# Graph layer with two branches: the first loads of x2 and adj cut finer, the warm-up shortened, and the opening lists of ScalarE and VectorE reordered

## What is computed

```python
def conv(x, a, eps, W, b):            # three layers
    ax = a @ x
    h = ax + (1.0 + eps[0]) * ax
    for i in range(3):
        h = relu(h @ W[i].T + b[i])
    return h
h = maximum(layernorm(x), 0.0)
out1 = conv(h,  adj, eps1, W1, b1)    # branch 0
out2 = conv(x2, adj, eps2, W2, b2)    # branch 1
return x + concatenate((out1, out2), axis=1) @ Wm.T + bm
```

## Time and profile before

| | |
|---|---|
| three runs | 405.01, 405.08, 406.11 us; median 405.08 |
| the profiled execution | 404.87 us, of which the traced span is 403.3 us |
| TensorE matmul | 399.4 us busy, 99% of the span, 1757 instructions |
| TensorE weight load | 327.0 us, 81% |
| VectorE, ScalarE | 219.6 us (54%), 220.4 us (55%) |
| DMA | 76.22 MB, mean 189 GB/s; above 400 GB/s in the first slices of the span |

### The profile page before, as it was taken

How to read it: one execution, slowest core, us unless ns; L and a number is a source line. 1 busy time by engine, 2 the same in 40 slices (tenths; PEclk the granted TensorE clock), 3 DMA queues, 4 the chain that set the end, 5 groups by cost and what they waited for, 6 DMA issues and landing times.

```text
span 403.3 us, 4833 instructions
## 1 busy us (share of the span) xinstructions
PE 399.4 (99%) x1757; PEld 327.0 (81%) x1757; DVE 219.6 (54%) x267; ACT 220.4 (55%) x258; POOL 8.4 (2%) x19
## 2 busy tenths in 40 slices
PE   8999999999999999999999999999999999999997
PEld 3788888888888888888888888888888888888886
DVE  5898878656464434551645517345373444755223
ACT  6876868557574533555433556334564335766034
POOL 0000000000000000000100001000000000000100
PEclk9999999999999999999999999999999999999999
DMA  8998883744645165334574336653175551740100
GB/s 301 420 403 338 310 327 142 297 154 152 236 154 198 53 244 203 108 119 197 172 296 160 119 137 228 240 207 132 76 260 208 208 193 42 264 179 2 52 0 28
DMA packets 14030, 76.22 MB, mean 189 GB/s; under 512 B 1920, under 2 KB 2176, under 8 KB 6080
## 3 DMA queue, kind: packets, MB, share of 16 engines
q1 hardware_dynamic: 12240, 71.18, 46.9%
q0 software_dynamic: 1200, 3.93, 2.9%
q10 hardware_dynamic: 576, 0.92, 0.7%
HBM read 73.93 MB, written 2.10 MB: 189 GB/s over the span
## 4 chain that ended last, share of the span: by engine, by line
PE 99%; DVE 0%; issue 0%; DVEq 0%
PE acc L590 24%; PE acc L586 24%; PE acc L587 24%; PE second_acc L587 3%; PE second_acc L586 3%; PE second_acc L590 3%; PE hidden L590 3%; PE hidden L586 3%; PE hidden L587 3%; PE second_acc L604 2%; PE acc L604 2%; PE merged L756 1%; PE acc L618 1%; PE merged L590 1%; PE merged L586 1%; PE merged L587 1%
## 5 line engine op out<-in xcount | busy, mean ns | idle before, releaser
L586 PE MATMUL acc<-adj_hi,feat_lo 128*128 128x512 f32 x432 | 168.0, 389 | 0.0
L587 PE MATMUL acc<-adj_hi,feat_hi 128*128 128x512 f32 x432 | 168.0, 389 | 0.0
L590 PE MATMUL acc<-adj_lo,feat_hi 128*128 128x512 f32 x432 | 168.0, 389 | 0.0
L423 DVE TENSOR_TENSOR adj_lo<-adj_raw,adj_hi 128x2048 fp32r<-128x2048 f32 x48 | 108.4, 2289 | 37.5 <-ACT adj_hi L264 36.6
L264 ACT ACTIVATE adj_hi<-adj_raw 128x2048 fp32r<-128x2048 f32 x48 | 90.3, 1924 | 17.3 <-PE acc L590 15.4
L429 DVE TENSOR_TENSOR act_lo<-act_f,act_hi 128x512 fp32r<-128x512 f32 x60 | 41.1, 691 | 104.4 <-ACT act_f L284 104.3
L587 PEld LDWEIGHTS acc<-adj_hi,feat_hi 128*128 128x128 f32 x432 | 81.1, 188 | 16.9
L590 PEld LDWEIGHTS acc<-adj_lo,feat_hi 128*128 128x128 f32 x432 | 81.1, 188 | 16.9
L586 PEld LDWEIGHTS acc<-adj_hi,feat_lo 128*128 128x128 f32 x432 | 81.1, 188 | 16.7
L283 ACT ACTIVATE act_hi<-hidden,bias 128x512 fp32r<-128x512 f32 x45 | 30.9, 688 | 95.5 <-PE hidden L590 95.5
L483 DVE TENSOR_TENSOR adj_lo<-adj_raw,adj_hi 128x2048 fp32r<-128x2048 f32 x14 | 31.7, 2290 | 5.4 <-ACT adj_hi L302 5.4
(11 more groups left out here) (82 smaller groups left out, 224.1 us busy)
## 6 DMA issues: line engine op xcount, KB each, us to landing
adj_raw<-adj_tiles SPq DMA_DIRECT2D x62, 1024.0 KB, 5.3
x_rows<-x_tiles SPq DMA_DIRECT2D x16, 256.0 KB, 7.3
x_res<-x_t POOLq DMA_DIRECT2D x8, 256.0 KB, 6.1
out_t<-y_sb POOLq DMA_DIRECT2D x7, 256.0 KB, 2.3
adj_raw<-adj_second SPq DMA_DIRECT2D x2, 512.0 KB, 6.5
adj_raw<-adj_first ACTq DMA_DIRECT2D x3, 256.0 KB, 4.4
w_raw<-w_t SPq DMA_DIRECT2D x1, 512.0 KB, 5.6
adj_raw<-adj_first SPq DMA_DIRECT2D x1, 256.0 KB, 5.0
```

Source lines behind the costliest of these rows:

```text
L423: nc.vector.tensor_tensor(adj_lo[:, u % RING, :], adj_raw[:, u % RING, :], f32(adj_hi[:, u % RING, :]), ALU.subtract).then_inc(lo_made, 1)
L586: nc.tensor.matmul(out, lhs_lo, rhs_hi, start=start, stop=False)
L587: nc.tensor.matmul(out, lhs_hi, rhs_hi, start=False, stop=False)
L590: return nc.tensor.matmul(out, lhs_hi, rhs_lo, start=False, stop=stop)
```

## The change

It cuts two of the first loads. Of x2's unit 0 the first block (128x128, 64 KB) gets a DMA and a semaphore of its own (`first_x2_loaded`), the other three blocks (192 KB) another. The first piece of adj is loaded in two halves by partitions, partitions 64 to 127 on SP's queue (`upper_loaded`), 0 to 63 on ScalarE's (`fine_loaded0`). x comes behind x2 on SP's queue, and the third piece of adj's first unit goes to ScalarE's queue, the fourth to SP's. Five of the twelve warm-up matmuls go. The lists of ScalarE and VectorE are reordered in the opening; the matmuls of TensorE keep their order, and the second of the raw ones now waits for the rest of x2.

```diff
--- before.py
+++ after.py
@@ -35,7 +35,7 @@
 
     PIECES = ((1, 1, 1, 1), (2, 2))
     X_SLOTS = 4
-    WARM_UP = 12
+    WARM_UP = 7
     HALF = JB // 2
 
 
@@ -131,6 +131,8 @@
         raw_loaded = [sem(f"raw_loaded{s}") for s in range(RING)]
         fine_loaded = [sem(f"fine_loaded{i}") for i in range(sum(len(p) - 1 for p in PIECES))]
         x_loaded = [sem(f"x_loaded{s}") for s in range(X_SLOTS)]
+        first_x2_loaded = sem("first_x2_loaded")
+        upper_loaded = sem("upper_loaded")
         x2_loaded = [sem(f"x2_loaded{s}") for s in range(X_SLOTS)]
         w_loaded = sem("w_loaded")
         bias_loaded = sem("bias_loaded")
@@ -214,9 +216,12 @@
                 sp.dma_start(x2_rows[:, u % X_SLOTS], x2_tiles[u]).then_inc(x2_loaded[u % X_SLOTS], 16)
 
 
+
+            sp.dma_start(x2_rows[:, 0, 0], x2_tiles[0, :, 0]).then_inc(first_x2_loaded, 16)
+            sp.dma_start(adj_raw[P // 2:P, 0, 0:CW], adj_first[0, P // 2:P]).then_inc(upper_loaded, 16)
+            sp.dma_start(x2_rows[:, 0, 1:JB], x2_tiles[0, :, 1:JB]).then_inc(x2_loaded[0], 16)
             load_x(0)
-            load_x2(0)
-            for s, i in ((0, 2), (1, 0), (1, 1)):
+            for s, i in ((0, 3), (1, 0), (1, 1)):
                 to, piece_of, done = piece_load(s, i)
                 sp.dma_start(to, piece_of).then_inc(done, 16)
             for s, (u, c) in enumerate(OPENING):
@@ -302,6 +307,8 @@
                 nc.scalar.activation(adj_hi[:, s % RING, :], adj_raw[:, s % RING, :], ACT.Copy).then_inc(hi_made, 1)
 
             def high_of_x2(u):
+                if u == 0:
+                    act.wait_ge(first_x2_loaded, 16)
                 act.wait_ge(x2_loaded[u % X_SLOTS], 16 * (u // X_SLOTS + 1))
                 nc.scalar.activation(feat_hi[:, 1, u * JB:(u + 1) * JB, :], x2_rows[:, u % X_SLOTS],
                                      ACT.Copy).then_inc(feat2_hi_made, 1)
@@ -332,26 +339,28 @@
                                      ACT.Copy).then_inc(feat1_hi_made, 1)
 
 
-            for i in (0, 1, 3):
+            act.dma_start(adj_raw[0:P // 2, 0, 0:CW], adj_first[0, 0:P // 2]).then_inc(fine_loaded[0], 16)
+            for i in (1, 2):
                 to, piece_of, done = piece_load(0, i)
                 act.dma_start(to, piece_of).then_inc(done, 16)
             act.wait_ge(constants_made, 2)
             nc.scalar.activation(root_of_zero[:, :], zero[:, :], ACT.Sqrt)
 
+            act.wait_ge(upper_loaded, 16)
             piece_high(0, 0)
-            std_of_x(0)
             piece_high(0, 1)
             high_of_x2(0)
+            std_of_x(0)
+            piece_high(0, 2)
+            piece_high(0, 3)
             act.wait_ge(rstd_made, 1)
             rectify_half(0, half_relu_made, half_feat1_made)
-            piece_high(0, 2)
-            piece_high(0, 3)
             rectify_half(1, relu_made, feat1_hi_made)
             piece_high(1, 0)
             piece_high(1, 1)
             high_of_x2(1)
+            high_of_opening(2)
             std_of_x(1)
-            high_of_opening(2)
             high_of_opening(3)
             rectify(1)
             for u in range(2, U - 2):
@@ -485,6 +494,8 @@
 
             def low_of_x2(u):
                 rows = slice(u * JB, (u + 1) * JB)
+                if u == 0:
+                    dve.wait_ge(first_x2_loaded, 16)
                 dve.wait_ge(x2_loaded[u % X_SLOTS], 16 * (u // X_SLOTS + 1))
                 dve.wait_ge(feat2_hi_made, u + 1)
                 nc.vector.tensor_tensor(feat_lo[:, 1, rows, :], x2_rows[:, u % X_SLOTS], f32(feat_hi[:, 1, rows, :]),
@@ -500,20 +511,21 @@
             nc.vector.memset(zero[:, :], 0.0).then_inc(constants_made, 1)
             nc.vector.memset(ln_eps[:, :], LN_EPS).then_inc(constants_made, 1)
 
+            dve.wait_ge(upper_loaded, 16)
+            piece_low(0, 0)
             variances(0)
+            piece_low(0, 1)
             scale_and_shift(0)
-            piece_low(0, 0)
-            piece_low(0, 1)
-            low_of_x2(0)
             piece_low(0, 2)
             piece_low(0, 3)
-            variances(1)
+            low_of_x2(0)
             low_of_x(0)
             piece_low(1, 0)
+            variances(1)
             piece_low(1, 1)
             low_of_x2(1)
+            low_of_opening(2)
             scale_and_shift(1)
-            low_of_opening(2)
             low_of_opening(3)
             low_of_x(1)
             for u in range(2, U - 2):
@@ -609,10 +621,14 @@
 
                 u, c = OPENING[s]
                 out = opening_bank(c, first)
-                pe.wait_ge(x2_loaded[u], 16)
+                if s == 0:
+                    pe.wait_ge(first_x2_loaded, 16)
+                    pe.wait_ge(upper_loaded, 16)
                 for i in pieces:
                     js, n = piece(s, i)
                     pe.wait_ge(raw_loaded[s] if n is None else fine_loaded[n], 16)
+                    if (s, i) == (0, 1):
+                        pe.wait_ge(x2_loaded[u], 16)
                     for j in js:
                         slot, cols = columns(s, j)
                         last = nc.tensor.matmul(out[:, :], x2_rows[:, u, j, :], adj_raw[:, slot, cols],
```

## The result

| | before | changed |
|---|---|---|
| median of 14 runs, us | 404.98 | 406.09 |
| lowest to highest | 404.67 to 406.11 | 405.55 to 406.35 |
| profiled execution, us | 404.87 | 406.17 |
| its span | 403.3 | 404.6 |
| TensorE matmul busy | 399.4 | 400.0 |

The ratio is 1.0022, 95% interval 1.0015 to 1.0029: 0.6 to 1.2 us slower, 0.9 in the middle (the medians stand 1.1 apart). That is less than the 0.3% I had set for a change, and more than the 0.1 us of the forecast.

The account below looks back on a forecast made before the run. TensorE bounds the kernel, 99% of the span. A 2.2 us earlier start leaves 1.1, spent waiting on x's late chain: 16.41 - 16.30 = +0.1 on 404.87 gives 405.0, plus 0.2 for the median, 405.2; range 404.0 to 406.2.

Parts of the forecast that it names:

- one named wait: TensorE's last two matmuls on chunk 1 wait for VectorE's second low: start at 16.41 instead of 16.30, +0.1 us.
- the working of 10.06 us: VectorE's chain from the start of x's statistics at 6.35 to TensorE's load behind the second low at 16.41.
- later lows: VectorE's lows after chunk 1: ready at 19.4 and 22.7, wanted at 20.3 and 23.0, so costed at nothing.
- the ring of adj: Slots for adj's loads, asked for at most 1 us later by SP, behind queued transfers: costed at nothing.
- The statistics start at 6.35.: VectorE's statistics of x, 4.29 before, wait for x behind 384 KB on SP's queue; bounds 6.1 and 7.3.
- The rival of the small transfers: Two additional issues hold x back 0.46 us each: statistics at 7.3, low at 17.35, time 406.1; chance 18%.
- I let the clock rise at the same instant: TensorE's clock goes from 1.2 to 2.4 GHz at about 6.65 as before, so the first split product could start at 10.55.
- the 1.1 us that the start was to leave: TensorE's raw matmuls start 2.2 us earlier; 1.1 is left at the first split product, the rest spent at the lower clock.
- Their data come in time.: adj's pieces for the raw matmuls: fourth in at 7.2, wanted 8.0; first half of chunk 1's unit 8.6, wanted 8.8.
- the first raw matmul: TensorE's first real work starts between 4.11 and 4.5, taken as 4.11, instead of 6.31.
- the clock rival: TensorE's clock stays low longer, time growing from a rise at about 9.1; all six raw matmuls slow gives 407.8; chance 9%.
- 1.2 us of TensorE standing: TensorE idle at L616 in pieces between 10.5 and 16.5, about 1.2 us in sum, the last released by VectorE's low.

Follow-up runs that it names:

- a_warm10: The changed kernel with 10 warm-up matmuls instead of 7: 405.72 us, ratio 1.0015 to the kernel before.
- a_adjwhole: The changed kernel with adj's first block in one load on ScalarE's queue: 405.00 us, ratio 0.9995 to the kernel before.
- a_stats: The changed kernel with the statistics of x's unit 1 moved behind the second low of chunk 1's unit: 405.33 us, ratio 1.0007 to the kernel before.
- s_whole_warm9: a_stats with both splits undone (x2's unit 0 and adj's first block whole), x2 before x, 9 warm-up matmuls: 405.09 us, ratio 0.9996.
- s_adjwhole: a_stats with adj's first block in one load on ScalarE's queue, x2's first block still by itself: 404.53 us, ratio 0.9985.
- s_cols: a_stats with adj's first block halved by columns instead of by partitions, one half on each queue: 405.55 us, ratio 1.0010.
- b_warm7: The kernel before with 7 warm-up matmuls and nothing else changed: 406.11 us, ratio 1.0015.
- s_x2whole: a_stats with x2's unit 0 in one load, adj's first block still in halves: 406.08 us, ratio 1.0022.
- s_oneq: a_stats with both halves of adj's first block on ScalarE's queue, one behind the other: 407.90 us, ratio 1.0068.
- a_warm10_stats: The changed kernel with 10 warm-up matmuls and the edit of a_stats together: 405.32 us, ratio 1.0001.

## Why the prediction was right and where it was wrong

**Right: the place and the mechanism.** The gain at the start was to be spent by x's late landing, through one named wait, and the time was to stay within 0.3%. In a_warm10 and a_adjwhole TensorE does stand in front of that load with VectorE's low as releaser, and the working of 10.06 us from the start of the statistics to the load measures 9.96 in both, and 9.95 in the changed kernel. (Its terms add up to 9.97; the rest is rounding on the way.) a_stats shows the wait by taking it away. What was costed at nothing (later lows, the ring of adj, the layers) cost nothing, by the last column of the table.

**Wrong, the size of one term: x's landing.** "The statistics start at 6.35." They started at 7.70, above the 7.3 that was its upper bound, and between 6.9 and 8.1 in the other kernels that kept adj's first block in two loads with one of them on SP's queue. Two parts of the working failed. The rate of the earlier trace rows was carried over to a queue that starts with smaller transfers: by 5.2 us 0.2 MB less were under way, and SP's queue had started x's last bytes by about 6.5, not 5.8. And the landing was put 0.55 behind the bytes, from one load in one execution; here it came 1.2 behind. The rival of the small transfers, 406.1 at 18%, is the nearest of the cases to the median, and s_whole_warm9 against s_adjwhole bears out that small loads cost more than their bytes. Its price came from the distances between SP's issues, and those are not the mechanism: x was issued 1.68 us later than before and came in 3.4 us later. The trace of a_adjwhole, with 512 KB on SP's queue up to and with x instead of 640, has 6.65, and the kernel's median is 405.00.

The Trainium skill (DMA: Bandwidth & Descriptors, Rules for kernel authors) says of two transfers to disjoint halves of the partitions that one should not bother, as both are spread over the same DMA engines. I had not weighed this rule, and it spoke against this part of the change. a_adjwhole agrees and goes further, with 1.1 us for the undoing of it: the half on SP's queue was in at 4.71 in the changed kernel, and the whole block at 4.12 in a_adjwhole. s_cols adds that halves by columns are no better.

**Wrong, one step: "I let the clock rise at the same instant."** In the profiled execution it rose after 8.8 us, which takes all of the 1.1 us that the start was to leave. The rival put the point from which it decides at 9.1, and the raw stage ended at 12.91, where it gave 14.4 for the case of all six. b_warm7 shows that fewer warm-up matmuls with a pause behind them cost 0.6 us by the ratio, by this alone. How often the clock is late in the changed kernel isn't settled; a_stats, with as few warm-up matmuls, shows a far outlying time in two of eleven runs, which speaks against its being what the median is made of.

**Wrong, one step that the wait for x hid: "Their data come in time."** The first half of chunk 1's unit was to be in at 8.6. It landed between 9.1 and 10.1 in the traced kernels with adj's first block in halves on the two queues, and x2's last three blocks kept the second raw matmul waiting as well. So with the clock up early, TensorE's first split product came at 11.65 in a_stats and in a_adjwhole and not at 10.55, and it asked for the low at 16.29 in a_stats and not at 15.2. The 1.1 us that x was to spend had been spent before. That the time was still within 0.3% owes something to luck: 406.09 is 0.1 us inside the upper end of the range, and three misses (x, the clock, the data) lay side by side and did not add up.

**Right with a small miss: the first raw matmul** at 4.0 to 4.5; it was 4.80, with 0.63 us of pause in front of it, the "some tenths" of the clock rival. Whether the pause made the clock late is not shown: the traces go both ways (see the last section).

**Not seen in this profile: 1.2 us of TensorE standing** at L616. The late clock filled that time with slow raw matmuls. a_warm10 has the picture that was forecast: its weight loads at L616 stand 0.43 and 0.33 us for ScalarE's rectified halves and at last 0.61 us for VectorE's low. a_adjwhole has the last of these alone, 0.35 us.

## What to carry to other kernels

When loads at the start are reordered, follow the operand that moved back through every engine to the instruction that waits for it, and price its landing from below and above, since a bandwidth read in one order does not hold for the first microseconds of another. Follow every other operand too: an engine that starts sooner asks sooner for all of its data. Cutting the first transfers finer made the first one land sooner (64 KB of x2 took 2.1 us from its issue in the changed kernel, 256 KB of x took 3.3 in the kernel before) and what stood behind them later; here the cut of adj's first block cost about 1 us and undoing it, with one statistics step moved behind the low that TensorE waits for, gave 404.53 us, ratio 0.9985 to the kernel before. Warm-up matmuls should about reach the first real work: five fewer of them with a pause of 1.3 us behind cost 0.6 us, while a pause of 0.3 us (s_adjwhole) cost nothing.

## What was not expected of the hardware

- The instant at which TensorE's clock rises differs between executions with the same seven warm-up matmuls. With a pause of 0.63, 1.28 and 1.0 us ahead of the first raw matmul (the changed kernel, b_warm7, s_x2whole) weight loads still took 0.34 us at 8.7 or later. With one of 1.13 us in s_oneq, and with 0.30 or less in s_adjwhole and a_adjwhole, a pair of loads took 0.30 us before 5.3, the upper level. In the kernel before, without a pause, loads took 0.19 from 6.81. So a pause and a late rise often came together here, and neither follows from the other in all traces.
- The same holds for the fall: a pause of 1.45 us came with it in s_oneq, and one of 1.43 us did not in a_adjwhole.
- The page and the stretches give the granted clock as 1.00 from the start, also where matmuls and weight loads take twice their time. The first rise is read from the durations, not from that row; the fall in s_oneq is in it.
- Loads of the same bytes on the same queue land up to 1.2 us apart from execution to execution: x's statistics began at 6.87 and at 8.09 in a_stats and a_warm10_stats, whose loads are identical.
